# A state-space layer's kernel spectrum, placed and transformed in two halves of heads

## Chip, cores, metric

One core of a Trainium2 chip. The metric is the device time of one execution in microseconds, median of the runs shown; lower is better.

## What is computed

Two layers over `x` of shape (4, 1024, 128). Layer 0 adds to `x` a long convolution (state-space kernel `K` of 128 heads, applied by FFT, then a layer norm) and a mixture of 8 experts with the top 2 per token; layer 1 adds an attention and a second mixture. The change lies in the first part of layer 0:

```python
dtA = exp(log_dt)[:, None] * (-exp(log_A_real) + 1j * A_imag)      # (128 heads, 64 states)
K = 2 * real(einsum('hn,hnl->hl', Ct, exp(dtA[:, :, None] * arange(1024))))
Xf = rfft(xn, n=2048, axis=1);  Kf = rfft(K, n=2048, axis=1)
y = irfft(Xf * Kf.T[None], n=2048, axis=1)[:, :1024]
out = layernorm(xn + y + xn * D) * ln_w + ln_b
x = x + out + experts(xn)           # silu(xn W1) * (xn W2) W3, top 2 of 8, gated
```

## The kernel before, in words

The program is written engine by engine; within an engine the order of the code is the order of execution, and semaphores (`wait_ge`, `then_inc`) tie the engines together. Nothing is reordered by a scheduler.

**Opening.** SyncE loads `x` in eight groups of rows; TensorE turns them, VectorE takes means and variances, ScalarE normalises (`xn`). VectorE picks each token's two experts; GpSimd scatters the token rows into slots sorted by expert (`x_slots`, 64 indirect stores) from 36 us on.

**Token spectra.** The convolution of length 1024 is done as transforms of two row groups (c = 0, 1) of 512 rows each. `spectra(n)`, n = 0 to 15, multiplies the table `fwd0` (loaded into `acc[:, 0:4]`) with two row tiles of 4 x 128 columns into one of four PSUM banks; `spectrum_copy(n)` on ScalarE moves it into `z`. Even and odd halves stand apart, and `spectrum_sums()` on VectorE later combines them, in 4 instructions for each of the two frequency groups m and the two row groups, 16 in all.

**Tables of K.** VectorE builds powers `low` and `high` by doubling, `doublings(0)` for heads of chunks 0 and 1 and `doublings(1)` for chunks 2 and 3. Between them it writes the low parts of the experts' weights (`w0_low(e)`), each after ScalarE's high part (`w0_high(e)`), each after SyncE's load into `wraw`, which again waits for a low part two experts earlier. TensorE multiplies chunk c of `high` and `low` (L1983, contraction of 64 rows, two row halves in turn), ScalarE copies the result into `k_out` (`k_copy(c)`). Ahead of chunk 2 stand 8 products on `ident` whose results nobody reads.

**Placing and transforming K.** When all four chunks are copied, TensorE brings K into time order with 16 products on the 0/1 matrix `place` (L1999: contraction of 32 rows, 256 columns, four products in a row on the same 32 rows). ScalarE copies to `k_t`, TensorE transforms with `fwd0` (`khat_product(n)`, n = 0 to 3, four products of 256 columns each), ScalarE copies to `khat`, VectorE combines (`khat_sums`, `khat_parts`).

**Chunks.** Behind this the first layer's experts run over 19 chunks of 512 tokens: per chunk `turn_inputs` (turn), `up` (L1897 to 1899, three products per fp32 pair of high and low parts), `Silu`, `hid`, `down` (L2040). The first `up(0, 0, 0)` needs `khat_product` issued, the turned tokens split by ScalarE (`input_high`) and VectorE (`input_low`), and the first weight load; SyncE's loads of tokens and weights start when `chunk_tables()` has written the chunk order (products L1991, `order_turned`). During the chunks VectorE works off 96 products of the spectra (`product(i)`) in 15 turns, share `2 * PAIR * n // TURNS`; SyncE's load of `inv` in turn 13 waits for 88 of them, and the pieces of layer 1's weights, which ScalarE splits before it copies the last chunk's output, come behind it on SyncE's queue.

## Time and profile before

| | us |
|---|---|
| median of 3 runs | 796.37 |
| lowest, highest | 796.05, 797.06 |
| the profiled execution | 795.81 |
| its span, first to last instruction | 794.1 |
| TensorE busy in it | 748.0 (94%) |
| VectorE busy | 663.9 (84%) |
| ScalarE busy | 544.6 (69%) |
| GpSimd busy | 144.1 (18%) |

The shares are over the whole span. The stages differ: TensorE is idle for long stretches before 92 us and busy without a gap in the chunk loop. In the rows, a matmul in fp32 counts as two records, and times are from the first instruction on.

### The profile page before, as it was taken

What the parts mean: (1) busy time and instruction counts of PE and PEld (TensorE: products, weight loads), DVE (VectorE), ACT (ScalarE), POOL (GpSimd) and SP (SyncE); (2) the same over time, 40 slices, a digit from 0 to 9 for tenths busy, and PEclk for the clock granted to TensorE, in tenths of its full rate; (3) what the DMA queues carried; (4) which work ended last, traced back from release to release, by engine and by line L of the source; (5) the groups of instructions that cost most, each with busy time, mean ns of one, the idle gap of its engine ahead of it and who ended that gap; (6) DMA issues with size and microseconds to landing.
All of it is one profiled execution on the core that took longest, in us unless ns stands there. A gap on an engine that the chain in (4) does not pass through costs nothing.

```text
span 794.1 us, 11901 instructions
## 1 busy us (share of the span) xinstructions
PE 748.0 (94%) x3911; PEld 602.1 (76%) x3911; DVE 663.9 (84%) x1591; ACT 544.6 (69%) x934; POOL 144.1 (18%) x138
## 2 busy tenths in 40 slices
PE   9694599999999979999999999999999999999998
PEld 4343478888886447678888888888888887999997
DVE  7899989999378799998999899869777679777775
ACT  5971244444343578788998899889999996756663
POOL 0177772000000716324070000000000000000000
PEclk9797899999999999999999999999999999999999
DMA  9884377898764106132233122122221100000000
GB/s 307 330 276 161 140 240 227 261 303 279 228 194 156 50 8 133 31 100 54 60 86 63 41 50 51 46 48 43 53 48 46 51 16 1 14 21 14 21 15 28
DMA packets 81277, 85.24 MB, mean 107 GB/s; under 512 B 7361, under 2 KB 59841, under 8 KB 80961
## 3 DMA queue, kind: packets, MB, share of 16 engines
q1 hardware_dynamic: 76672, 75.93, 32.9%
q0 software_dynamic: 4096, 8.40, 3.7%
q8 instruction: 31, 0.51, 0.3%
q14 instruction: 30, 0.24, 0.1%
q10 hardware_dynamic: 448, 0.17, 0.1%
HBM read 59.17 MB, written 25.30 MB: 106 GB/s over the span
## 4 chain that ended last, share of the span: by engine, by line
PE 73%; DVE 19%; issue 2%; ACT 2%; DMA 2%; POOL 1%; SPq 0%; DVEq 0%; POOLq 0%; ACTq 0%
PE ps L1897 20%; PE ps L1899 19%; PE ps L1898 19%; PE ps L2040 5%; PE ps L2264 3%; DVE hid_lo L1823 2%; DVE xn L1498 1%; PE ps L2291 1%; POOL gate_row L685 1%; PE ps L2019 1%; PE ps L2010 1%; DMA wraw<-w 1%; DVE stats L988 1%; ACT xn L722 1%; DMA wst<-w 1%
## 5 line engine op out<-in xcount | busy, mean ns | idle before, releaser
L1823 DVE TENSOR_TENSOR hid_lo<-hid,hid_hi 128x512 fp32r<-128x512 f32 x256 | 175.9, 688 | 44.7 <-ACT hid_hi L912 41.8
L911 ACT ACTIVATE hid<-ps,b_sb 128x512 f32<-128x512 f32 x256 | 176.7, 690 | 45.1 <-PE ps L1899 25.5
L912 ACT ACTIVATE hid_hi<-ps,b_sb 128x512 fp32r<-128x512 f32 x256 | 174.7, 682 | 0.0
L1897 PE MATMUL ps<-hid_hi,w_lo 128*128 128x512 f32 x256 | 101.4, 396 | 5.3 <-DVE hid_lo L1823 5.3
L1897 PE MATMUL ps<-xt_hi,w_lo 128*128 128x512 f32 x256 | 102.3, 400 | 1.8 <-DVE xn L1490 1.8
L1899 PE MATMUL ps<-xt_hi,w_hi 128*128 128x512 f32 x256 | 100.0, 390 | 0.0
L1899 PE MATMUL ps<-hid_hi,w_hi 128*128 128x512 f32 x256 | 99.8, 390 | 0.0
L1898 PE MATMUL ps<-xt_lo,w_hi 128*128 128x512 f32 x256 | 99.7, 389 | 0.0
L1898 PE MATMUL ps<-hid_lo,w_hi 128*128 128x512 f32 x256 | 99.7, 389 | 0.0
L820 ACT ACTIVATE act<-ps 128x512 f32<-128x512 f32 (+1 forms) x57 | 34.0, 596 | 75.1 <-PE ps L1899 75.0
L685 POOL DMA_INDIRECT u_both<-y_slots,slot x56 | 64.7, 1155 | 85.4 <-DVE hid_lo L1823 69.6
L662 POOL DMA_INDIRECT x_slots<-xn,slot x64 | 69.1, 1080 | 53.1 <-DVE pairs L1177 33.9
L1897 PEld LDWEIGHTS ps<-hid_hi,w_lo 128*128 128x128 f32 x256 | 48.0, 188 | 21.1 <-DVE hid_lo L1823 11.1
L2040 PEld LDWEIGHTS ps<-wd,hid 128*128 128x128 f32 (+1 forms) x456 | 58.1, 191 | 3.7
L2040 PE MATMUL ps<-wd,hid 128*128 128x128 f32 (+1 forms) x456 | 59.7, 274 | 0.0
L706 ACT ACTIVATE pt_hi<-ps 128x512 fp32r<-128x512 f32 x64 | 35.0, 598 | 35.3 <-PE ps L2264 35.3
L1332 DVE TENSOR_TENSOR hid<-act,ps 128x512 f32<-128x512 f32 (+1 forms) x57 | 39.0, 683 | 22.1 <-ACT act L820 21.8
L1897 PEld LDWEIGHTS ps<-xt_hi,w_lo 128*128 128x128 f32 x256 | 48.1, 188 | 11.8 <-DVE xn L1490 2.2
L1899 PEld LDWEIGHTS ps<-xt_hi,w_hi 128*128 128x128 f32 x256 | 48.1, 188 | 10.4
L1899 PEld LDWEIGHTS ps<-hid_hi,w_hi 128*128 128x128 f32 x256 | 48.0, 188 | 10.4
L1815 DVE TENSOR_REDUCE sm<-ps 128x1 f32<-128x1024 f32 x32 | 39.2, 1224 | 19.6 <-PE ps L1899 19.2
L1898 PEld LDWEIGHTS ps<-hid_lo,w_hi 128*128 128x128 f32 x256 | 48.1, 188 | 9.5
(367 smaller groups left out, 1530.6 us busy)
## 6 DMA issues: line engine op xcount, KB each, us to landing
gate_row<-gates_dram SPq DMA_DIRECT2D x64, 256.0 KB, 4.9
wc<-w_split SPq DMA_DIRECT2D x57, 256.0 KB, 3.3
w_split<-wc SPq DMA_DIRECT2D x8, 768.0 KB, 4.4
x_slots<-prod SPq DMA_DIRECT2D x11, 512.0 KB, 7.6
xc<-x_slots SPq DMA_DIRECT2D x19, 256.0 KB, 3.6
y_slots<-yo SPq DMA_DIRECT2D x19, 256.0 KB, 3.1
wst<-w SPq DMA_DIRECT2D x16, 256.0 KB, 4.4
wd<-w SPq DMA_DIRECT2D x19, 192.0 KB, 4.4
```

The source lines that it names most:

```text
L662: nc.gpsimd.indirect_dma_start(x_slots, bass.IndirectOffsetOnAxis(ap=slot[:, k, t:t + 1], axis=0), rows_of_tile(t), None).then_inc(block_i ...
L685: nc.gpsimd.indirect_dma_start(dst, None, y_slots, rows_of).then_inc(signal, 16)
L706: copy = lambda dst, src: nc.scalar.activation(dst, src, ACT.Copy)
L911: nc.scalar.activation(hid1[:, u % 4], ps[:, u % 4], ACT.Gelu_apprx_tanh, bias=b1_sb[:, u:u + 1])
L912: nc.scalar.activation(hid1_hi[:, u % 4], ps[:, u % 4], ACT.Gelu_apprx_tanh, bias=b1_sb[:, u:u + 1]).then_inc(hid1_done, 1)
L1332: tt(hid[0:f, j], act[0:f, r], ps[0:f, 2 + r], mul).then_inc(hid_done, 1)
L1815: v = step.mark(nc.vector.reduce_max(sm[:, s, 0:1], ps[:, 2 * (n % 2):2 * (n % 2) + 2].rearrange("p a w -> p (a w)"), AX.X))
L1823: tt(hid1_lo[:, u % 4], hid1[:, u % 4], hid1_hi[:, u % 4].bitcast(F32), sub).then_inc(hid1_lo_done, 1)
L1897: mm(dst, a_lo, b_hi, start=first, stop=False)
L1898: mm(dst, a_hi, b_lo, start=False, stop=False)
L1899: return mm(dst, a_hi, b_hi, start=False, stop=last)
L2040: last = mm(ps[:, 4 + s, tokens], hid[0:f, j, tokens], wd[0:f, s, j * P:(j + 1) * P], start=(j == 0 and t == 0), stop=(j == J0 - 1 and t = ...
```

## The change

K is placed and transformed in two halves d = 0, 1 of 64 heads each. The host orders the heads so that chunks 0 and 1 are the heads 0 to 63, chunks 2 and 3 the rest. TensorE's new order: spectra 0 to 13, chunks 0 and 1, spectra 14 and 15, `place_product(0)`, the four `khat_product(0, n)`, chunk 2, the products of the chunk order, chunk 3, `place_product(1)`, the four `khat_product(1, n)` with the first `turn_inputs` after the first of them. Each placing or transforming product has 128 columns instead of 256, and the placing loop now has the row block `a` innermost. `k_t` moves to `acc[:, 6:8]`.

The spectra of the second row group (n = 8 to 15) take four row tiles instead of two; for one of the two halves some of the tables are the negated ones in `minus0`, a new input of 0.5 MB, loaded behind `fwd0`. So their even and odd parts come out combined, and `spectrum_sums(0)` on VectorE does the first row group alone. The 8 products on `ident` are gone. VectorE fills `place` behind `doublings(0)`. The share of products per turn is `min(13 * n // 2, 96)`, and GpSimd waits for an arrived block one tile earlier.

```diff
-                if t % BT == 1 and t > BT:
+                if t % BT == 0 and t:
                     block_arrived(t // BT - 1)
...
             sp.dma_start(fwd0, dft_fwd).then_inc(fwd0_in, 16)
+            sp.dma_start(minus0, dft_minus).then_inc(fwd0_in, 16)
...
+            k_t_copy(0)
+            act_e.wait_ge(w0_lo_done, E)
+            for n in range(M):
+                khat_copy(0, n)
+            k_copy(2)
+            k_copy(3)
+            k_t_copy(1)
...
-            def spectrum_sums():
+            def spectrum_sums(row_group):
 
                 dve.wait_ge(spectra_copied, 16)
-                for c in range(2):
+                for c in (row_group,):
...
-                upto_turn = lambda n: 2 * PAIR * n // TURNS
+                upto_turn = lambda n: min(13 * n // 2, 2 * PAIR)
...
-                    for i in range(2):
-                        t = 2 * odd + i
-                        last = mm(for_batch(ps[:, n % 4]), fwd0[:, t, part_, m * P:(m + 1) * P], rows3(c * CT + t),
-                                  start=(i == 0), stop=(i == 1))
+                    tiles = (0, 1, 2, 3) if c == 1 else (2 * other, 2 * other + 1)
+                    for t in tiles:
+                        from_minus = c == 1 and other and t // 2 != part_
+                        table = minus0[:, t % 2] if from_minus else fwd0[:, t]
+                        last = mm(for_batch(ps[:, n % 4]), table[:, part_, m * P:(m + 1) * P], rows3(c * CT + t),
+                                  start=(t == tiles[0]), stop=(t == tiles[-1]))
...
+            def place_product(d):
+                pe.wait_ge(k_copied, 4 * d + 4)
+                pe.wait_ge(spectra_copied, 16)
+                pe.wait_ge(place_done, 1)
+                if d:
+                    pe.wait_ge(khat_copied, M)
+                    pe.wait_ge(slots_done, 5)
+                for i in range(HG):
+                    for a in range(HG):
+                        block = slice(a * LO, (a + 1) * LO)
+                        last = mm(ps[:, a, d * P:(d + 1) * P], place[block, (3 - i) * LO:(7 - i) * LO],
+                                  k_out[block, d * 2 * G:(d + 1) * 2 * G, a * LO + i * G:a * LO + (i + 1) * G],
+                                  start=(i == 0), stop=(i == HG - 1))
...
             for c in range(KC):
                 if c == 2:
-                    pe.wait_ge(k_copied, 4)
-                    pe.wait_ge(spectra_copied, 16)
-                    for _ in range(8):
-                        mm(ps[:, 0, 0:2 * P], ident[:], fwd0[:, 0, 0, 0:2 * P], start=True, stop=True)
+                    spectra(range(SPECTRA_FIRST, 16))
+                    place_product(0)
+                    for n in range(M):
+                        khat_product(0, n)
+                if c == 3:
+                    pe.wait_ge(order_done, 1)
+                    pe.wait_ge(khat_copied, M)
+                    for i in range(3):
+                        last = mm(ps[0:1, 0, i * NC:(i + 1) * NC], of_chunk[:, i:i + 1], order_f[:], start=True, stop=True)
+                    last.then_inc(order_turned, 1)
```

The order of instructions at three places follows; line numbers are those of each kernel's own text. TensorE from ahead of chunk 2 (`ps<-high,low`) on, before:

```order
L1974 MATMUL ps<-acc,ident 128x256 [waits spectra_copied,k_copied]
L1974 MATMUL ps<-acc,ident 128x256 x7
L1983 MATMUL ps<-high,low 128x128 [waits k_copied,tables_done]
L1983 MATMUL ps<-high,low 128x128 x15
L1983 MATMUL ps<-high,low 128x128 [waits k_copied,tables_done]
L1983 MATMUL ps<-high,low 128x128 x15
L1991 MATMUL ps<-order_f,of_chunk 1x23 [waits k_copied,order_done]
L1991 MATMUL ps<-order_f,of_chunk 1x23 x2
L1999 MATMUL ps<-prod,place 128x256 [waits spectra_copied,k_copied,place_done]
L1999 MATMUL ps<-prod,place 128x256 x15
L2010 MATMUL ps<-half_way,acc 128x256 [waits k_t_copied]
```

The same place now (`prod` holds `k_out`, the second operand of L2014 lies in `acc` like the first):

```order
L2001 MATMUL ps<-prod,place 128x128 [waits place_done,spectra_copied,k_copied]
L2001 MATMUL ps<-prod,place 128x128 x15
L2014 MATMUL ps<-acc 128x128 [waits k_t_copied]
L2014 MATMUL ps<-acc 128x128 x15
L2038 MATMUL ps<-high,low 128x128 [waits k_copied,tables_done]
L2038 MATMUL ps<-high,low 128x128 x15
L2028 MATMUL ps<-order_f,of_chunk 1x23 [waits khat_copied,order_done]
L2028 MATMUL ps<-order_f,of_chunk 1x23 x2
L2038 MATMUL ps<-high,low 128x128 [waits k_copied,tables_done]
L2038 MATMUL ps<-high,low 128x128 x15
L2001 MATMUL ps<-prod,place 128x128 [waits khat_copied,place_done,slots_done,spectra_copied,k_copied]
L2001 MATMUL ps<-prod,place 128x128 x15
```

One half of placing and transforming moved ahead of chunk 2, and the products of the chunk order moved between chunks 2 and 3.

ScalarE from the copy of spectrum 6 (`z<-ps`) on, with the high parts of experts 4 to 7 (`wc<-wraw`), before:

```order
L706 ACTIVATE z<-ps 128x512 [waits spectra_mm] x10
L706 ACTIVATE wc<-wraw 128x3x256 [waits w0_stored0,wraw_in0]
L706 ACTIVATE wc<-wraw 128x3x256 [waits w0_stored1,wraw_in1]
L706 ACTIVATE wc<-wraw 128x3x256 [waits w0_stored0,wraw_in0]
L706 ACTIVATE wc<-wraw 128x3x256 [waits w0_stored1,wraw_in1]
L706 ACTIVATE prod<-ps 128x512 [waits k_mm_done,spare_out,blanks_out]
L706 ACTIVATE prod<-ps 128x512 [waits k_mm_done] x7
L706 ACTIVATE half_way<-ps 128x2x32x8 [waits k_t_done] x2
```

And now:

```order
L709 ACTIVATE z<-ps 128x512 [waits spectra_mm] x2
L709 ACTIVATE wc<-wraw 128x3x256 [waits w0_stored0,wraw_in0]
L709 ACTIVATE z<-ps 128x512 [waits spectra_mm]
L709 ACTIVATE wc<-wraw 128x3x256 [waits w0_stored1,wraw_in1]
L709 ACTIVATE z<-ps 128x512 [waits spectra_mm] x5
L709 ACTIVATE prod<-ps 128x512 [waits k_mm_done,spare_out,blanks_out]
L709 ACTIVATE prod<-ps 128x512 [waits k_mm_done] x3
L709 ACTIVATE wc<-wraw 128x3x256 [waits w0_stored0,wraw_in0]
L709 ACTIVATE z<-ps 128x512 [waits spectra_mm]
L709 ACTIVATE wc<-wraw 128x3x256 [waits w0_stored1,wraw_in1]
L709 ACTIVATE z<-ps 128x512 [waits spectra_mm]
L709 ACTIVATE acc<-ps 128x4x16x8 [waits k_t_done]
```

The high parts of experts 6 and 7 now stand behind the copies of chunks 0 and 1, that of expert 7 also behind the copy of spectrum 14.

VectorE in turn 13 of the chunk loop, from the chunk's third `hid` (85 rows) to its next chunk's second; products 86 and 87, counted from 0, are the pair `z<-prod`. Before:

```order
L1332 TENSOR_TENSOR hid<-act,ps 85x512 [waits act_done]
L1379 TENSOR_TENSOR prod<-z,khat 128x512 [waits products_done]
L1383 TENSOR_TENSOR prod<-prod 128x512 [waits products_done]
L1331 ISA
L1332 TENSOR_TENSOR hid<-act,ps 128x512 [waits act_done]
L1383 TENSOR_TENSOR prod<-prod 128x512 [waits products_done]
L1387 TENSOR_TENSOR z<-prod 128x512 [waits products_done] x2
L1331 REGISTER_ALU
L1332 TENSOR_TENSOR hid<-act,ps 128x512 [waits act_done]
```

And now:

```order
L1355 TENSOR_TENSOR hid<-act,ps 85x512 [waits act_done]
L1406 TENSOR_TENSOR prod<-prod 128x512 [waits products_done] x2
L1354 ISA
L1355 TENSOR_TENSOR hid<-act,ps 128x512 [waits act_done]
L1410 TENSOR_TENSOR z<-prod 128x512 [waits products_done] x2
L1387 TENSOR_TENSOR z<-z 128x512 [waits products_done]
L1354 REGISTER_ALU
L1355 TENSOR_TENSOR hid<-act,ps 128x512 [waits act_done]
```

The pair moved one product nearer to the `hid` ahead of it.

## Rows read from the trace of the kernel before

**Rows 1.** Chain of waits, 60 to 120 us: start, duration, what, records.
```profile
82.44 1.83 DVE wc L1222 x2
...
91.21 0.70 DVE high L1303
91.96 3.84 PE ps L1983 x64
...
97.02 4.89 PE ps L1999 x32
101.93 1.08 ACT half_way L706
103.06 1.99 PE ps L2010 x8
105.05 0.44 PE ps L2019 x4
105.49 5.18 PE ps L2010 x24
```

**Rows 2.** Stages: window, length, busy by engine with records, granted clock, DMA share, GB/s.
```profile
62.30:70.90 8.60, 0.00 (x0) 0.00 (x1) 8.53 (x16) 2.06 (x3) 6.46 (x8) 0.76 0.14 46
70.90:77.00 6.10, 6.07 (x56) 6.10 (x58) 5.96 (x33) 0.00 (x0) 4.88 (x5) 0.50 0.82 272
...
87.30:92.00 4.70, 2.19 (x12) 1.58 (x11) 4.67 (x10) 0.00 (x0) 3.48 (x5) 1.00 0.40 136
...
121.00:160.00 39.00, 39.00 (x251) 33.75 (x250) 38.08 (x63) 17.73 (x33) 3.11 (x3) 1.00 0.84 248
230.00:246.00 16.00, 16.00 (x102) 13.67 (x101) 15.55 (x27) 7.00 (x13) 0.00 (x0) 1.00 0.46 132
```

**Rows 3.** Timeline of TensorE: start, duration, line, operands, records, idle before and releaser.
```profile
51.70 10.57 PE L1952 MATMUL ps<-xn,acc 128*128 128x512 f32 x24 [0.60 <-ACT z L706]
70.93 6.71 PE L1983 MATMUL ps<-high,low 64*128 64x128 f32 x64 [8.66 <-issue]
...
95.73 0.31 PE L1991 MATMUL ps<-order_f,of_chunk 128*1 128x23 f32 x6
...
110.32 0.58 PE L1897 MATMUL ps<-xct_hi,wc 128*128 128x512 f32 x1
```

**Rows 4.** Timelines of VectorE, SyncE's queue and ScalarE, end of the chunk loop.
```profile
243.36 1.29 DVE L1387 TENSOR_TENSOR z<-prod 128x512 f32<-128x512 f32 x2
244.67 0.34 SPq L569 DMA_DIRECT2D prod<-dft_inv  x1
251.99 0.63 ACT L706 ACTIVATE w_hi<-wst 128x512 fp32r<-128x512 f32 x1 [4.84 <-DMA wst<-w]
```

**Rows 5.** Timeline of VectorE around the end of the tables.
```profile
93.88 0.24 DVE L1212 TENSOR_SCALAR order_f<-consts,place_f 128x23 f32<-128x23 f32 x1
...
94.38 0.38 DVE L1442 TENSOR_REDUCE place<-ident 128x32 f32<-128x128 f32 x1
...
97.12 0.68 DVE L1342 TENSOR_TENSOR z<-z 128x512 f32<-128x512 f32 x1
...
107.41 0.69 DVE L1327 TENSOR_TENSOR xct_lo<-ps,xct_hi 128x512 fp32r<-128x512 f32 x1
```

**Rows 6.** Timeline of ScalarE: the high part of expert 7, the last copies to `k_out`.
```profile
81.47 0.84 ACT L706 ACTIVATE wc<-wraw 128x768 fp32r<-128x768 f32 x1 [3.50 <-DMA wraw<-w]
...
95.83 1.09 ACT L706 ACTIVATE prod<-ps 128x512 f32<-128x512 f32 x2 [0.70 <-PE ps L1983]
```

**Rows 7.** Timeline of SyncE's queue: the load of expert 7, the first weights.
```profile
73.58 0.50 SPq L501 DMA_DIRECT2D wraw<-w  x1
...
101.26 1.39 SPq L528 DMA_DIRECT2D wc<-w_split  x3
```

**Rows 8.** DMA view, 0 to 130 us: transfer, count, KB each, median us to landing.
```profile
wc<-w_split SPq DMA_DIRECT2D x14, 256.0 KB, 3.6
...
acc<-dft_fwd SPq DMA_DIRECT2D x1, 1024.0 KB, 9.8
```

More of the change, by code:

```diff
@@ L42 @@
 STATIC_PAIRS = MIN_PAIRS - 2
+SPECTRA_FIRST = 14
 TURNS = 1 + 2 * STATIC_PAIRS + 4
@@ L730, in spectrum_copy @@
             def spectrum_copy(n):
-                c, m, part_, odd = spectrum(n)
+                c, m, part_, other = spectrum(n)
                 act_e.wait_ge(spectra_mm, n + 1)
-                copy(z[:, m + HM * odd, c, part_], ps[:, n % 4]).then_inc(spectra_copied, 1)
+                copy(z[:, m + HM * other, c, part_], ps[:, n % 4]).then_inc(spectra_copied, 1)
             def w0_high(e):
@@ L1315, in _ @@
             doublings(0)
+            dve.wait_ge(ident_done, 1)
+            dve.wait_ge(ranked, 1)
+            v = step.mark(nc.vector.memset(place[:], 0.0))
+            need(v)
+            nc.vector.reduce_sum(place[:, 3 * LO:4 * LO], ident.rearrange("p (a n) -> p n a", a=HG), AX.X).then_inc(place_done, 1)
             w0_low(4)
@@ L1436, in weights_low @@
                 tt(w_lo[:, col:col + cols], wst1[:, n % STAGES, 0:cols], w_hi[:, col:col + cols].bitcast(F32), sub).then_inc(w1_lo_done, 1)
-            dve.wait_ge(ident_done, 1)
-            dve.wait_ge(ranked, 1)
-            v = step.mark(nc.vector.memset(place[:], 0.0))
-            need(v)
-            nc.vector.reduce_sum(place[:, 3 * LO:4 * LO], ident.rearrange("p (a n) -> p n a", a=HG), AX.X).then_inc(place_done, 1)
             chunk_tables()
             gates0()
-            spectrum_sums()
+            spectrum_sums(0)
             dve.wait_ge(rows_in, 80)
@@ L1942, in spectra @@
                 for n in numbers:
-                    c, m, part_, odd = spectrum(n)
+                    c, m, part_, other = spectrum(n)
                     if n >= 4:
@@ L1965, in _ @@
             mm(ps[:, 7, 0:T * E], before[:], chosen, start=False, stop=True).then_inc(ranked, 1)
-            pe.wait_ge(fwd0_in, 16)
-            spectra(range(16))
+            pe.wait_ge(fwd0_in, 32)
+            spectra(range(SPECTRA_FIRST))
             pe.wait_ge(ws_lo_done, 1)
+            k_halves = k_t.rearrange("p (c t) h -> p t c h", c=2)
+            def place_product(d):
[11 more added lines that the diff above has]
+                                  start=(i == 0), stop=(i == HG - 1))
+                        if i == HG - 1:
+                            last.then_inc(k_t_done, 1)
@@ new lines, in khat_product @@
+            def khat_product(d, n):
+                m, odd = divmod(n, 2)
+                bank, at = khat_at(d, n)
+                if n == 0:
+                    pe.wait_ge(k_t_copied, d + 1)
+                for part_ in range(2):
+                    for i in range(2):
+                        last = mm(ps[:, bank, at + part_ * P:at + (part_ + 1) * P], fwd0[:, 2 * odd + i, part_, m * P:(m + 1) * P],
+                                  k_halves[:, 2 * odd + i, :, d * HH:(d + 1) * HH], start=(i == 0), stop=(i == 1))
+                last.then_inc(khat_mm, 1)
@@ L1985, in _ @@
                                 last.then_inc(k_mm_done, 1)
[L1988 to L2013 removed]
+            place_product(1)
             def turn_inputs(q, k, s):
```

99 lines of the change are left out of this document (40 added, 59 removed).

## Prediction

> **What bounds the kernel now.** I read the chain of waits first, over the stretch from 60 to 112 us, because every line of the diff but one acts there. Up to 91.91 us it runs through VectorE: the doubling tables of the second 32 heads, with the splits of the expert weights between them [rows 1]. VectorE has no gap there that matters (5.96 of 6.10 us busy, 8.53 of 8.60 [rows 2]). From 91.96 us it is a ladder on which TensorE and ScalarE take turns: products of chunks 2 and 3 (3.84), copies, placing (4.89), copy (1.08), transform (1.99 and 5.18 with the turning of the first tokens, 0.44, between), and at 110.32 us the first expert product [rows 1, 3]. That is 18.4 us in which one engine waits for the other. The second thing to see is that TensorE has nothing to do for long stretches ahead of the ladder: no instruction from 62.3 to 70.9 us, and a granted clock of 0.50, the 1.2 GHz level, when it starts again [rows 2]. The third is what comes behind: from 121 to 160 us TensorE is busy 39.00 of 39.00 us [rows 2], so whatever time the ladder gives back moves the whole chunk loop forward. Last I read the end of the loop, 230 to 246 us, where VectorE is busy 15.55 of 16.00 us [rows 2] and a load that waits for its products leads to the last output and the first gather [rows 4].
>
> **The ladder, step by step.** The change does half of the placing and transforming (heads of chunks 0 and 1) before the last tables are ready, so behind them only the other half stands. I follow the new ladder from its start to the first expert product, which was at 110.32.
>
> Start. VectorE's two instructions that fill `place` move from behind `order_f` to ahead of the weight split of experts 4 and 5. They run from 94.12 to 94.76 [rows 5], so they cost 0.64 us on the bounding engine: the tables end at 92.55 and TensorE starts at 92.60 instead of 91.96.
>
> Products of chunks 2 and 3. They took 3.84 us for 64 records, 0.060 each [rows 1]. Chunk 2 ends at 92.60 + 1.92 = 94.52. Now the three small products for the chunk order stand between the chunks and wait for `order_f`, which was ready at 93.88 + 0.24 = 94.12 [rows 5] and is now at 94.76. Six records of theirs start within 0.2 us or so (six took 0.31 with the tail of the last [rows 3]), so chunk 3 runs from 95.0 to 96.9. The wait holds up only TensorE; what is queued behind it is chunk 3, and behind that everything on the ladder. It costs 0.5 us, and in return the tables for SyncE come about 0.9 us earlier.
>
> Copies to `k_out`. From the end of the products to the first placing product it was 95.80 to 97.02, 1.22 us with two copies of 1.09 in all [rows 1, 6]. The same now: 98.1.
>
> Placing. Before: 16 products with 256 columns, 32 records, 4.89 us, 0.153 each [rows 1]; four products in a row use the same 32 rows of the array. Now 16 products with 128 columns, and neighbours use different row groups. No row shows that. One bound is a strictly serial pace: a transform record with 256 columns takes 7.17 / 32 = 0.224 us [rows 1], so one with 128 columns 0.112, and 32 of them 3.6 us. The nearest row is that of the `k` products, the same 128 columns and two row groups in turn, 0.060 a record, so 1.92 us. The other bound is four groups at once, 3.6 / 4 = 0.9 us. I take 1.92, since shape and alternation are those of that row: placing ends at 100.0.
>
> On this the Trainium skill speaks too (TensorEngine Tiling (Array Packing), Performance Considerations and Key Properties): a contraction of 32 rows or fewer can go four tiles wide, since tiles load weights and multiply independently. By that the step would be 0.9 us and the sum 1.0 us better; no row here shows four groups, so I keep two. The same section speaks against the change: a change of the tiling mode drains the engine, and the new order switches between 64, 128 and 32 rows oftener. The row at 95.73 differs: the 128-row products follow the 64-row products with no idle time recorded before them [rows 3]. By the row it costs nothing; were there a drain it would add to the ladder.
>
> Copy to `k_t`. One ScalarE copy of 512 elements a partition was exposed behind the placing, 101.93 to 103.06 with its hand-overs, 1.13 [rows 1]. The new copy has 512 elements too: 101.2.
>
> Transform. 32 records of 0.224 us and 0.44 for the turning made 103.06 to 110.32 [rows 1, 3]. Now half the columns: 3.58 + 0.44 = 4.0, so the first expert product can start at 105.2. Its inputs: VectorE's `xct_lo` stood at 107.41, behind 16 `spectrum_sums` that begin at 97.12 [rows 5], ready but never late. Had those 16 stayed, `xct_lo` would now end near 107 and hold TensorE by 2 us; with the eight of row group 0 VectorE is free near 102. So that part of the change gives nothing by itself and is what lets the rest through. The gain at the first expert product is 110.32 - 105.2 = 5.1 us: -2.97 placing, -3.26 transform, +0.64, +0.5.
>
> **What has to be hidden.** TensorE now has to finish the first half before 92.60. Spectra 8 and up have four products, eight records at 0.44 us [rows 3] instead of four: spectrum 9 ends near 54.6, 13 near 68.7. So the idle time ahead of 70.93 shrinks from 8.6 to about 2.2 us; a pause of 2.5 us inside 87.3 to 92.0 left the clock at 1.00 [rows 2]. At that clock chunks 0 and 1 take 3.84 and not 6.71 us [rows 1, 3]: 74.8. Spectra 14 and 15 are 3.52 each: 78.3 and 81.8. ScalarE copies 15 only after the split of expert 7, whose load it had to wait for until 81.47 [rows 6] and which is 0.64 later now: 83.0, copied 83.6. Placing 1.92, copy 1.13, transform 3.58: 90.2. The cover is 2.4 us; beyond it each microsecond costs one. VectorE wants the split of expert 7 at about 84.0 (second of the two at 82.44 plus 0.64 [rows 1]); margin 1.0. The eight products on `ident` ahead of chunk 2 go, at no price. The new 0.5 MB load of `minus0` follows the 1 MB of `fwd0`, which landed 9.8 us after its issue among other loads [rows 8]; half as much data is 0 to 5 us more by that row, and the first spectra wait for it. I take 1, because it queues behind the same loads as `fwd0`; that comes out of the 2.2 us ahead of 70.93, and from there on each microsecond goes into the cover of 2.4. Weights: the first load was issued at 101.26 [rows 7] and lands in 3.6 us [rows 8]; 0.9 earlier that is 104.0, against a need at 105.2.
>
> **The end of the loop.** The share of the spectrum products becomes 13n//2 a turn. In turn 13 the product that the load of `inv` waits for, number 88, comes as second behind the middle `hid` and not as third, so SyncE's 244.67 comes 0.60 us earlier (VectorE does two in 1.29 with the tail of the second), and with it the piece of weights that ScalarE waits 4.84 us for until 251.99, the last output behind that piece and the gather [rows 4]. Between 0 (were the piece late for another reason) and 1.2 us (two products); I take 0.6. That GpSimd waits for a landed block one tile earlier I price at nothing, since no step of the ladder waits for GpSimd [rows 1]; were the first token load late for it, that would take from the 1.2 us that the weights have left.
>
> **The sum.** 5.1 + 0.6 = 5.7 us. The profiled execution took 795.81 us, 794.1 of it span; it would be 790.1. It lies 0.56 under the median of the three runs, 796.37, and I forecast for the median: 796.37 - 5.7 = 790.7.
>
> **Rivals.**
> A. Placing runs four row groups at once: 1.0 less, 789.7. For it: 32 rows; against: no row shows more than two at once.
> B. Part of the gain is not there: placing stays serial (+1.7, 792.4), or the first weights come late. The load issued at 73.58 was waited for until 81.47, 7.9 us [rows 6, 7]; one like it would hold the first product by 3 us, 793.7.
> C. The gain goes into a new wait: `minus0` or the loads of experts 6 and 7 come so late that tables and first half end 4 to 6 us later, 795 to 797. Against it: the margins of 1.0 to 2.4 us above, and traffic of the same size as before from 70 to 83 us.
> D. Slower: TensorE does the first half at 1.2 GHz. Chunks 0 and 1 then end at 77.6 as in the row, spectrum 14 at 84.7, so ScalarE's split of expert 7, now queued behind its copy, ends at 86.1 and VectorE stands; spectrum 15 ends at 91.7, placing at 96.2, copy at 97.3, transform at 104.5, 11.9 us past 92.60: 790.7 + 11.9 = 802.6. It costs from 2.4 us on and is slower than before from 5.7 us past 92.60 on. For it: the clock was 0.50 for 6 us at this place [rows 2]. Against it: that followed 8.6 us without work, which is filled now, and the clock rose within 6 us of work.
>
> **How the numbers follow.** Forecast 0.62, A 0.10, B 0.14, C 0.08, D 0.06. Faster by over 0.2% (1.6 us, about what a measurement of this kernel tells from no change) are the forecast, A, B and a little of C: 0.88. Within 0.2%: most of C, 0.06. Slower: D, 0.06. The range goes from 789.0 (A with the upper end of the tail) to 793.4 (B with serial placing and 1 us of a missed cover); C and D, 0.14, and the worst of B lie outside.
>
> **What would show it.** In the changed profile: placing as two stretches, the second about 1.9 us long; the second transform 4.0 us with the turning; the last tables at 92.6; the first expert product at 105; granted clock 1.00 from 70.9; SyncE's `inv` load 5.7 us earlier. The forecast is wrong if the first half ends after 92.6, if `xct_lo` or a weight load is what the first expert product waits for, or if the chunk loop shows new idle time on TensorE.

## Result, and the profile after

The changed kernel takes 790.3 us (median of 4 runs, 789.29 to 790.4) against 796.21 us of the kernel before on the same chip (4 runs, 795.25 to 797.06): a ratio of 0.9917, 95% interval 0.9896 to 0.9938. I had forecast 790.7. The sum is right to half a microsecond, but its two terms are not: counted alike, the ladder gave less than I had worked out and the end of the loop three times as much.

The profiled execution's span is 788.6 us; before it was 794.1. TensorE in the stretch of the ladder, its timeline, columns as in [rows 3]:

```profile
72.06 3.84 PE L2038 MATMUL ps<-high,low 64*128 64x128 f32 x64 [2.57 <-issue]
75.84 7.13 PE L1972 MATMUL ps<-xn,acc 128*128 128x512 f32 x16
83.92 1.17 PE L2001 MATMUL ps<-prod,place 32*128 32x128 f32 x32 [0.95 <-issue]
86.34 3.84 PE L2014 MATMUL ps<-acc 128*128 128x128 f32 x32 [1.25 <-ACT acc L709]
93.74 2.68 PE L2038 MATMUL ps<-high,low 64*128 64x128 f32 x32 [3.56 <-DVE high L1321]
96.36 0.39 PE L2028 MATMUL ps<-order_f,of_chunk 128*1 128x23 f32 x6
96.68 2.86 PE L2038 MATMUL ps<-high,low 64*128 64x128 f32 x32
100.71 1.17 PE L2001 MATMUL ps<-prod,place 32*128 32x128 f32 x32 [1.17 <-ACT prod L709]
103.15 1.16 PE L2014 MATMUL ps<-acc 128*128 128x128 f32 x8 [1.27 <-ACT acc L709]
104.15 0.60 PE L2048 MATMUL ps<-ident,xc 128*128 128x128 f32 x4
104.58 2.84 PE L2014 MATMUL ps<-acc 128*128 128x128 f32 x24
107.18 0.48 PE L1915 MATMUL ps<-xct_hi,wc 128*128 128x512 f32 x1
```

The shape is the forecast one: the first half of placing and transform lies ahead of chunk 2, with 3.56 us to spare, chunks 0 and 1 take 3.84 us and not 6.71 [rows 3], and the second placing and transform are short. Against it stand chunks 2 and 3: 2.68 and 2.86 us for 32 records each, where 1.92 were due. The stages show why (columns as in [rows 2]):

```profile
90.20:93.70 3.50, 0.00 (x0) 0.00 (x0) 3.46 (x8) 0.38 (x1) 2.58 (x4) 1.00 0.24 75
93.70:95.00 1.30, 1.26 (x22) 1.26 (x24) 1.26 (x12) 0.00 (x0) 0.99 (x2) 0.99 0.20 63
95.00:98.40 3.40, 3.40 (x38) 3.09 (x36) 2.38 (x16) 1.09 (x2) 2.70 (x3) 0.50 0.19 60
98.40:99.60 1.20, 1.14 (x20) 0.95 (x18) 1.20 (x3) 0.03 (x1) 0.98 (x1) 1.00 0.17 55
```

TensorE has no work from 90.2 to 93.7 us, and from 95.0 to 98.4 its granted clock is 0.50, the 1.2 GHz level.

The two executions also began differently, which hides part of the gain. VectorE's write of the tokens' slots, which ends the routing and comes ahead of every line of the diff that matters here, stands 1.23 us later in the changed kernel. The timeline of the kernel before, TensorE and VectorE:

```profile
6.27 1.02 PE L1913 MATMUL ps<-prod,wg_centred 128*8 128x512 f32 x2
...
35.28 0.20 DVE L1169 CAST slot<-slot_f 128x64 int32<-128x64 f32 x1
```

and that of the changed kernel:

```profile
6.73 1.88 PE L1931 MATMUL ps<-prod,wg_centred 128*8 128x512 f32 x2
...
36.51 0.20 DVE L1187 CAST slot<-slot_f 128x64 int32<-128x64 f32 x1
```

The same two products of the routing took nearly twice as long, which is what the lower clock makes of the products of chunks 0 and 1 elsewhere; the rows give 1.00 for this first stretch in both profiles, so I read the pace from the durations. It comes with the execution: one program below (the version with unused products as fillers) has this write at 36.41 us in one profile and at 35.22 in the other. How often each kernel starts late is not shown: the three profiles of the kernel before and of a version of it have the write at 34.9 to 35.3, the two of the changed kernel at 36.5, and versions of the changed kernel at both. So I count from that write on (us behind it; "due" is the prediction's own ladder, less 35.28; the last column, e11, is the version without fillers at the end of the experiments):

| | before | due | changed | e11 |
|---|---|---|---|---|
| last tables end | 56.63 | 57.27 | 57.18 | 56.49 |
| products of chunk 3 end | 60.52 | 61.62 | 63.03 | 60.83 |
| placing ends | 66.62 | 64.72 | 65.37 | 63.17 |
| first expert product | 75.04 | 69.92 | 70.67 | 68.47 |
| load of `inv` on SyncE | 209.39 | 203.67 | 204.33 | 202.13 |
| first Gelu of the next part | 248.40 | 242.70 | 242.21 | 239.85 |
| end | 758.77 | 753.07 | 752.13 | 749.89 |

The rows of the tail, the changed kernel's load of `inv` and first Gelu (timelines of SyncE's queue and ScalarE), then the first Gelu of the kernel before:

```profile
240.84 0.34 SPq L572 DMA_DIRECT2D prod<-dft_inv  x1
278.72 0.67 ACT L929 ACTIVATE hid<-ps,b_sb 128x512 f32<-128x512 f32 x1
```

```profile
283.68 0.67 ACT L911 ACTIVATE hid<-ps,b_sb 128x512 f32<-128x512 f32 x1
```

Like for like the two profiles differ by 6.6 us: 4.4 up to the first expert product, 0.7 from there to the load of `inv`, 1.1 from that load to the first Gelu, and 0.4 behind it, for which no cause was looked for.

### The profile page after: what moved, and what is told of

Read it like the earlier page. It is cut to its first block, busy times and chain, and to the rows that moved or that the text cites. A ratio compares the mean times of both kernels' runs of the same rounds, so it can differ in the third digit from the quotient of the medians.

```text
span 788.6 us, 12059 instructions
## 1 busy us (share of the span) xinstructions
PE 756.0 (96%) x3991; PEld 603.6 (77%) x3991; DVE 658.5 (83%) x1583; ACT 544.5 (69%) x938; POOL 145.3 (18%) x138
## 4 chain that ended last, share of the span: by engine, by line
PE 75%; DVE 16%; DMA 3%; ACT 2%; issue 2%; POOL 1%; SPq 0%; DVEq 0%; ACTq 0%; POOLq 0%
PE ps L1915 20%; PE ps L1917 20%; PE ps L1916 20%; PE ps L2069 6%; PE ps L2291 3%; DVE hid_lo L1841 2%; DVE xn L1516 1%; PE ps L1931 1%; PE ps L2318 1%; PE ps L2048 1%; POOL gate_row L688 1%; DMA wraw<-w 1%; ACT xn L725 1%; PE ps L2038 1%; DVE wc L1240 1%
## 5 line engine op out<-in xcount | busy, mean ns | idle before, releaser
L665 POOL DMA_INDIRECT x_slots<-xn,slot x64 | 71.1, 1111 | 55.9 <-DVE pairs L1195 35.1
L709 ACT ACTIVATE pt_hi<-ps 128x512 fp32r<-128x512 f32 x64 | 35.0, 598 | 35.3 <-PE ps L2291 35.3
L1355 DVE TENSOR_TENSOR hid<-act,ps 128x512 f32<-128x512 f32 (+1 forms) x57 | 38.9, 682 | 21.4 <-ACT act L840 21.0
L1833 DVE TENSOR_REDUCE sm<-ps 128x1 f32<-128x1024 f32 x32 | 39.1, 1223 | 19.6 <-PE ps L1917 19.2
```

The costliest lines, as they stand in the source:

```text
L665: nc.gpsimd.indirect_dma_start(x_slots, bass.IndirectOffsetOnAxis(ap=slot[:, k, t:t + 1], axis=0), rows_of_tile(t), None).then_inc(block_i ...
L709: copy = lambda dst, src: nc.scalar.activation(dst, src, ACT.Copy)
L1355: tt(hid[0:f, j], act[0:f, r], ps[0:f, 2 + r], mul).then_inc(hid_done, 1)
L1833: v = step.mark(nc.vector.reduce_max(sm[:, s, 0:1], ps[:, 2 * (n % 2):2 * (n % 2) + 2].rearrange("p a w -> p (a w)"), AX.X))
```

## Experiments

**Is it the pause ahead of chunk 2?** The eight products on `ident` that the change takes away ahead of chunk 2, priced by me at nothing, could have kept the clock up. Seven of them, called fillers below, were put back behind the first half:

```
                     for n in range(M):
                         khat_product(0, n)
+                    for _ in range(7):
+                        mm(ps[:, 7, 0:2 * P], ident[:], fwd0[:, 0, 0, 0:2 * P], start=True, stop=True)
```

> Seven products of 256 columns on the identity (results unused, to a PSUM bank that is free there) stand on TensorE behind the first half's transform and ahead of chunk 2, where the changed kernel is idle from 90.2 to 93.7 us and then runs the products of chunks 2 and 3 from 95.0 to 98.4 at a granted clock of 0.50. Theory: the idle time is what brought the clock down, and the eight products that the change removed from this place, which I had priced at nothing, kept it up. Then with the seven the clock stays at 1.00, chunk 2 takes 1.92 us instead of 2.62, chunk 3 1.92 instead of 2.85, and the first expert product comes 1.2 to 1.6 us earlier (with a start like that of the changed kernel's profile near 105.7 instead of 107.18): 790.3 - 1.4 = 788.9. Rival 1: the slow pace comes from the three products of the order between the chunks and the turn from 64 to 128 and back to 64 rows; then pace and time stay (790.3). Rival 2: the clock falls all the same, the seven only delay chunk 2: 790.3 to 791.

Measured: 790.61 us (789.26 to 791.2), no gain over 790.3. The theory is half right. TensorE's timeline and its stages in this run:

```profile
93.61 2.06 PE L2040 MATMUL ps<-high,low 64*128 64x128 f32 x32 [0.52 <-DVE high L1321]
96.00 0.31 PE L2030 MATMUL ps<-order_f,of_chunk 128*1 128x23 f32 x6 [0.34 <-DVE order_f L1230]
96.24 2.06 PE L2040 MATMUL ps<-high,low 64*128 64x128 f32 x32
99.46 1.17 PE L2001 MATMUL ps<-prod,place 32*128 32x128 f32 x32 [1.17 <-ACT prod L709]
101.91 2.08 PE L2014 MATMUL ps<-acc 128*128 128x128 f32 x8 [1.27 <-ACT acc L709]
```

```profile
101.40:104.80 3.40, 2.89 (x13) 2.89 (x14) 1.32 (x3) 0.46 (x1) 2.49 (x4) 0.50 0.86 263
```

The chunks run at full pace (2.06 with the tail of the last record), so the products of the order were not what slowed them. But the stretch of 0.50 is still there, 6.4 us later, behind two pauses of 1.2 us in which TensorE waits for ScalarE's copies, and it now slows the transform: the first 8 records take 2.08 us and not 1.16. It also shows the wait for `order_f` that the slow clock hides in the changed kernel: 0.34 us.

**Placing over the row groups in turn, or one after the other.**

```
-                for i in range(HG):
-                    for a in range(HG):
+                for a in range(HG):
+                    for i in range(HG):
```

> Only the order of the 16 placing products is put back: four in a row on the same 32 rows, then the next 32. Theory: the second placing took 1.17 us (32 records, 0.037 each) because neighbours lie in four different row groups; in series a record of 128 columns is half of the 0.153 of 256 columns to 0.112, so 2.4 to 3.6 us, and the first expert product comes 1.2 to 2.4 us later: 791.5 to 792.7. The first half has 3.5 us of cover and hides its own part. Rival: the placing was short because it has 128 columns and not because of the row groups; then it stays near 1.2 to 1.6 and the time at 790.3 to 790.7.

Measured: 792.82 us (791.95 to 795.36). The second placing in its timeline:

```profile
98.99 2.98 PE L2001 MATMUL ps<-prod,place 32*128 32x128 f32 x32 [1.17 <-ACT prod L709]
```

2.98 us against 1.17, but the last 0.47 us of it lie in a stretch of 0.50 that starts at 101.5 us. The first placing of the same run had the clock at 1.00 throughout:

```profile
83.70 2.79 PE L2001 MATMUL ps<-prod,place 32*128 32x128 f32 x32 [1.17 <-issue]
```

So at the same clock the order over the four row groups is worth 1.6 us, a factor of 2.4. The stretch also takes in the transform, so the first expert product is 2.6 us later (73.30 behind the routing) and not 1.6 to 1.8. By the Trainium skill (TensorEngine Tiling (Array Packing), Theoretical Speedup) the gain of 32-row tiles is up to four times. The runs show 2.4. The Trainium skill also names a drain at a change of the tiling mode (same page, Key Properties). The timelines show no idle time for it between 64-row and 128-row products (96.24 above).

**The same order alone, in the kernel before.**

```
-            for a in range(HG):
-                block = slice(a * LO, (a + 1) * LO)
-                for i in range(HG):
+            for i in range(HG):
+                for a in range(HG):
+                    block = slice(a * LO, (a + 1) * LO)
...
-                if a % 2:
-                    last.then_inc(k_t_done, 1)
+                    if i == HG - 1 and a % 2:
+                        last.then_inc(k_t_done, 1)
```

> The kernel before with one line's order changed: the 16 placing products go over the four row groups in turn, as in the changed kernel; no halves, no negated tables, nothing moved. It tells what this order alone is worth. Theory: 32 records of 256 columns at twice the changed kernel's 0.037 us take 2.3 to 2.4 us instead of 4.89. But both copies to k_t, of which the first lay beside the placing, now stand behind it, 1.08 us more, so the first expert product comes about 1.5 us earlier: 796.4 - 1.5 = 794.9. Rival: it stays at 4.9 us, since 256 columns fill the array's columns whatever the rows: no gain, or 1 us lost by the copy, 797.5.

Measured: 794.63 us (793.64 to 797.27), beside 797.81 for the kernel before, measured with it (795.47 to 801.26); ratio 0.9959, interval 0.9936 to 0.9981. Placing took 2.01 us, a factor of 2.4 for 256 columns too, and the copy behind it costs about what was expected (TensorE waits 2.06 us, before 1.16, so 0.9 of the expected 1.08):

```profile
96.89 2.01 PE L1999 MATMUL ps<-prod,place 32*128 32x256 f32 x32 [0.98 <-issue]
100.95 3.68 PE L2010 MATMUL ps<-half_way,acc 128*128 128x256 f32 x8 [2.06 <-ACT half_way L706]
```

In the profiled execution a stretch of 0.50 from 101.0 to 104.4 ate most of the gain (first expert product 74.65 us behind the routing, before 75.04); in the median the one line is worth 3.2 us, by the interval 1.5 to 5.1.

**Half the sums on VectorE.** The last step of my ladder rests on VectorE being free in time because TensorE now does the second row group's sums.

```
-                for c in (row_group,):
+                for c in range(2):
```

> VectorE does the sums of both row groups again, 16 instead of 8, over the spectra that TensorE has already combined (so the second row group is summed twice and its spectrum is another one); TensorE's work stays. It prices the VectorE side of the negated tables. In the changed kernel VectorE is free at 102.9 and xct_lo runs at 105.48, 1.1 us before the first expert product can need it. Theory: eight more sums of 0.60 us end at 107.7, xct_lo ends at 108.4, and TensorE's second product, which needs it, starts 1 us or a little more later: first to third expert product later by 0.9 to 1.3 us, time 791.2 to 791.6. The khat sums behind them come 2.2 us later and hold nothing. Rival: the spectrum products in the chunk loop, of which VectorE has 38.0 of 39.0 us full, come later by 4.8 us and never catch up, and the loop's end comes later too: 793 to 795. Rival: no effect, 790.3, if something else holds TensorE until 108.

Measured: 793.1 us (791.57 to 794.54). `xct_lo` follows the sums without a gap and TensorE waits for it; VectorE, then TensorE:

```profile
106.45 0.68 DVE L1370 SCALAR_TENSOR_TENSOR z<-z 128x512 f32<-128x512 f32 x1
107.06 0.28 DVE L1465 TENSOR_SCALAR vec_rows<-vec_rows 128x128 f32<-128x128 f32 x1
107.37 0.69 DVE L1350 TENSOR_TENSOR xct_lo<-ps,xct_hi 128x512 fp32r<-128x512 f32 x1
```

```profile
108.11 0.50 PE L1915 MATMUL ps<-xct_hi,wc 128*128 128x512 f32 x1 [1.00 <-DVE xct_lo L1350]
```

Up to here it costs the expected microsecond; counted from the routing 0.7 are left, since this run's tables came 0.5 us earlier. Up to its end the run loses 1.75 us against the changed kernel (753.88 against 752.13): another 0.3 in the chunk loop, 0.3 behind the load of `inv`, 0.4 behind the first Gelu. The median lies 2.5 us above that of the run with the seven products, measured beside it. So it is 1 us at the place and 2 or a little more in all; what makes the rest was not taken apart.

This run also bears on the pause ahead of chunk 2, which was 2.68 us in it and not 3.56. The clock fell all the same, from 94.9 to 98.3 us:

```profile
93.41 2.48 PE L2038 MATMUL ps<-high,low 64*128 64x128 f32 x32 [2.68 <-DVE high L1321]
```

**What the longer spectra do for the clock.** The other side of the same edit:

```
-                    tiles = (0, 1, 2, 3) if c == 1 else (2 * other, 2 * other + 1)
+                    tiles = (2 * other, 2 * other + 1)
```

> TensorE's spectra of the second row group have two tiles each again, without the sums that belong to it (the second row group's even and odd parts stay uncombined, so its spectrum is another one); VectorE's work stays. It tells what the longer spectra do for the clock. Theory: TensorE is then idle from about 63.5 to 72 us, chunks 0 and 1 run at a granted clock of 0.50 as in the kernel before (6.7 us instead of 3.84). They end near 78.8; spectra 14 and 15 are 1.8 us each instead of 3.5, so the copy of spectrum 15 still waits for the split of expert 7 (load until 82.5) and the first half ends near 90.2 to 91 as now, inside the 3.5 us of cover: 790.3. Rival (D of the prediction): the clock falls again behind chunks 0 and 1, as it did at 80.4 us in the kernel before, placing and transform run at half pace (2.3 and 7.7 us instead of 1.17 and 3.84) and the first half ends near 95.3: 1.6 us past the tables, 791 to 792.5, less what a warm clock in chunks 2 and 3 then gives back.

Measured: 790.24 us (789.27 to 792.56), the changed kernel's time. TensorE's timeline:

```profile
70.97 6.68 PE L2038 MATMUL ps<-high,low 64*128 64x128 f32 x64 [9.25 <-issue]
...
84.31 2.09 PE L2001 MATMUL ps<-prod,place 32*128 32x128 f32 x32 [3.02 <-issue]
...
92.81 2.06 PE L2038 MATMUL ps<-high,low 64*128 64x128 f32 x32
```

This is rival D in a milder form: the clock is at 0.50 from 66.7 to 77.0 and again from 83.8 to 90.6 us, chunks 0 and 1 take 6.68 us and the first placing 2.09. Yet chunk 2 starts only 0.5 us behind its tables, since the clock comes back in between and the cover is larger than I had it. I had priced D at 11.9 us by letting the low level hold from 70.9 to the end of the first half, and with spectra twice as long. With these two-tile spectra it costs 0.5. With the long ones the low level was met here for 3.4 us only (70.7 to 74.1, in a profile with fillers below), and the first half still ended ahead of the tables.

**The share of the spectrum products in a turn.**

```
-                upto_turn = lambda n: min(13 * n // 2, 2 * PAIR)
+                upto_turn = lambda n: 2 * PAIR * n // TURNS
```

> Only the share of the spectrum products in each turn of the chunk loop is put back. It prices the term of the tail. From the first expert product to SyncE's load of inv the changed kernel took 0.69 us less than the kernel before (133.66 against 134.35 us), and from there to the first Gelu of the next part 1.1 us less. Theory: the 0.6 us come from the pair of products that moved one place forward, so here the first stretch is 134.3 us again, while the rest of the tail, the weight piece and the gathers, does not depend on it: 790.3 + 0.6 = 790.9. Rival: the whole tail hangs on it, by the time at which the gathers meet other transfers: 134.3 and 39.0 us, 791.9.

Measured: 790.78 us (one run), 134.30 us from the first expert product to the load of `inv` and 38.98 from there to the first Gelu: the rival holds. The time is only half a microsecond above the changed kernel's because this execution started early (the write of the slots at 34.98 us). Counted from the routing it ends 1.9 us later (754.04 against 752.13), 1.7 of them between the first expert product and the first Gelu, for an edit of which I had the price at 0.6. GpSimd's gathers of the first outputs, in the timeline of this run and then of the changed kernel's second profile:

```profile
256.23 1.44 POOL L688 DMA_INDIRECT gate_row<-y_slots,slot  x1 [0.30 <-issue]
257.97 1.49 POOL L688 DMA_INDIRECT gate_row<-y_slots,slot  x1 [0.30 <-issue]
259.77 0.94 POOL L688 DMA_INDIRECT gate_row<-y_slots,slot  x1 [0.30 <-issue]
```

```profile
256.90 0.94 POOL L688 DMA_INDIRECT gate_row<-y_slots,slot  x1 [0.30 <-issue]
258.14 0.94 POOL L688 DMA_INDIRECT gate_row<-y_slots,slot  x1 [0.30 <-issue]
```

Two of the eight gathers are half a microsecond longer, and each of the two lies over a 128x512 instruction of VectorE with two operands from SBUF (this run, VectorE):

```profile
255.57 1.28 DVE L1459 TENSOR_TENSOR w_lo<-wst,w_hi 128x512 fp32r<-128x512 f32 x2
...
257.99 0.66 DVE L1550 TENSOR_TENSOR xn<-xn,vec_rows 128x512 f32<-128x512 f32 x1
```

The Trainium skill (GPSIMD Engine Reference, Specifications) says that GpSimd shares its SBUF interfaces with VectorE and names VectorE instructions with two SBUF inputs among those that contend. The rows agree in what they pair; but in the second profile of the changed kernel the gather at 256.90 lies over the same instruction and stays at 0.94, so what decides is finer than an overlap. VectorE there:

```profile
256.29 1.33 DVE L1459 TENSOR_TENSOR w_lo<-wst,w_hi 128x512 fp32r<-128x512 f32 x2
```

Read instruction by instruction, the fourth gather of all fourteen profiles sorts itself by when a `w_lo` starts beside it. Where one starts 0.02 to 0.07 us ahead of the gather, the gather takes 1.43 to 1.48 us (five profiles). Where one starts within 0.01 us of it, the gather takes 0.94 or 0.95 us and that `w_lo` 0.71 to 0.73 instead of 0.68 (three). Where one starts 0.10 to 0.35 us behind it, the gather takes 1.00 to 1.25 us (six). This is a pattern of the rows; no run took the collision by itself.

**The kernel before once more, and the changed kernel once more.**

> The kernel before once more, for a second profile of it: how much of the difference between the two profiles is chance. Theory: the start up to the end of the routing (35.28 us before, 36.51 in the changed kernel) differs between executions of one kernel by a microsecond, because the granted clock rises at another time; from the end of the routing to the first expert product it is 75.0 us again, from that to the load of inv 134.35 again. From that load to the first Gelu it was 39.0 us and 37.9 in the changed kernel: if that is the change's, 39.0 again; if it is chance of the gathers, anything from 37.8 to 39. Time 795 to 797.

> The changed kernel once more, for a second profile. Theory: TensorE's granted clock falls to 0.50 for 3.4 us or more somewhere between 85 and 106 us, since all six kernels with the unfilled pauses of the ladder showed that (at 95.0, 101.4, 87.9 and 101.5, 94.9, 100.9, 92.8 us), and its place differs from execution to execution; the first expert product comes 70 to 73 us behind the end of the routing (70.7 in the first profile). From the first expert product to the load of inv 133.67 us again. Time 790.3. Rival: the stretch at 95.0 to 98.4 is fixed by the program and is there again, within a tenth of a microsecond of the start of chunk 2.

Measured: 799.56 us (one run) and 790.34 us (790.24 to 790.57). The changed kernel repeats to a tenth: start 36.50, a stretch of 0.50 from 94.8 to 98.2, first expert product 70.73 us behind the routing, 133.67 to the load of `inv`; my expectation that the stretch wanders was wrong for this kernel. The kernel before doesn't repeat. Its second profile has a stretch of 0.50 from 99.6 to 109.8 us, where the first had none:

```profile
96.30 6.34 PE L1999 MATMUL ps<-prod,place 32*128 32x256 f32 x32 [0.97 <-issue]
```

Placing took 6.34 and not 4.89 us [rows 1], the first expert product comes at 79.13 us behind the routing and not 75.04. From there to the load of `inv` it is 134.36 again, and from that to the first Gelu 39.13 (39.01 in the first). So the profile on which I built the sum was a lucky one: four medians of the kernel before, taken at different times, are 796.2, 797.3, 796.4 and 797.8 us, its runs lie from 794.8 to 801.3, while the eight runs of the changed kernel lie between 789.3 and 790.6.

**All pauses filled, and a version to beat both.** Two of the fillers also behind chunk 3 and two behind the second placing:

> Beside the seven products on the identity ahead of chunk 2, two of them stand behind chunk 3 and two behind the second placing, where TensorE waits 1.2 us each time for a copy of ScalarE. With the seven alone the stretch at a granted clock of 0.50 did not go away but moved from 95.0 to 98.4 on to 101.4 to 104.8, from the products of chunks 2 and 3 on to the transform, so the time stayed. Theory: the pauses of the ladder taken together bring the clock down, and with all three filled it stays at 1.00 to the first expert product, which then comes 1.3 to 1.6 us earlier than in the changed kernel, measured from the end of the routing (70.7 us behind it there, 69.2 now): 790.3 - 1.4 = 788.9. Rival: the stretch of 0.50 moves on once more, behind the first expert product or into it, and the time stays at 790.3. Rival: the fillers end late and delay what follows by up to 0.3 us each.

Measured: 790.16 us (788.09 to 793.53). The profiled execution is the slowest of the four and shows what fillers can't mend:

```profile
85.52 2.07 PE L2001 MATMUL ps<-prod,place 32*128 32x128 f32 x32 [2.28 <-issue]
88.81 5.55 PE L2014 MATMUL ps<-acc 128*128 128x128 f32 x32 [1.22 <-ACT acc L709]
94.19 3.19 PE L2025 MATMUL ps<-acc,ident 128*128 128x256 f32 x14
97.31 2.06 PE L2040 MATMUL ps<-high,low 64*128 64x128 f32 x32
```

The load of expert 7 came later here, the first placing waited 2.28 us for it, the clock fell to 0.50 from 85.6 to 92.4, and the first half ended level with the tables; the fillers then held chunk 2 for another 3.2 us.

The version has six, two and two fillers and three further edits: the fill of `place` ahead of `w0_low(0)`, where VectorE waits for ScalarE anyway, the order's products one quarter into chunk 3, and on SyncE the second token load behind the first expert's weights.

```
+            v = step.mark(nc.vector.memset(place[:], 0.0))
...
             w0_low(0)
...
+                    if c == 3 and i == 1:
+                        pe.wait_ge(order_done, 1)
...
-            for q in range(2):
-                x_load_early(q, q)
+            x_load_early(0, 0)
...
                 down_load(e, q)
+                if q == 0:
+                    x_load_early(1, 1)
```

> A version to beat both kernels: the fillers of the run before (six, two and two products), the two instructions that fill place at the head of VectorE's weight splits where it waits 1.3 us for ScalarE, the order's three products one quarter into chunk 3 (so that TensorE does not wait for order_f), and on SyncE the second token load behind the first expert's weights. Theory: 0.64 us for place, 0.3 for the order, 1.4 for the clock: first expert product 68.3 us behind the end of the routing instead of 70.7, time 790.3 - 2.4 = 787.9. Rival: the first weights become the wait; they land near 103 us of the profile, earlier by 1.7 us through the order on SyncE, else they would have been level with the need. Rival: the clock falls in the ladder all the same: 789.3.

> The version with filled pauses, place set up early, the order inside chunk 3 and the weights first, once more beside the changed kernel on the same chip. Theory: no stretch of 0.50 in the ladder, first expert product 68.3 us behind the end of the routing again, time 1 to 2 us under the changed kernel's of the same call. Rival: that its first profile had no such stretch was chance; then a stretch is there, and the time is within 0.8 us of the changed kernel's.

> The same version without the fillers: place set up early, order inside chunk 3, weights first. It tells the fillers' part. Theory: a stretch of 0.50 of 3.4 us or more is in the ladder again and costs 1.3 to 1.7 us; first expert product 69.6 to 70.1 us behind the end of the routing against 68.3 with the fillers, time 0.9 us under that of the changed kernel. Rival: the other three edits carry it all: 68.3 again.

Measured: 789.27 us (788.34 to 789.59) at first; later, all on one chip, 788.06 (787.56 to 788.61) with the fillers, 787.89 (786.94 to 791.25) without, and 790.34 for the changed kernel. So the version is 2.3 us faster than the changed kernel, and by the medians of four runs each the fillers are not what does it. Without them, TensorE's timeline in the profiled execution, the fastest of the four:

```profile
91.84 2.50 PE L2039 MATMUL ps<-high,low 64*128 64x128 f32 x40 [2.98 <-DVE high L1322]
94.27 0.31 PE L2032 MATMUL ps<-order_f,of_chunk 128*1 128x23 f32 x6
94.51 1.61 PE L2039 MATMUL ps<-high,low 64*128 64x128 f32 x24
97.28 1.17 PE L2002 MATMUL ps<-prod,place 32*128 32x128 f32 x32 [1.17 <-ACT prod L710]
```

and its stage:

```profile
91.80:103.80 12.00, 9.52 (x139) 8.97 (x139) 10.08 (x40) 4.88 (x9) 9.26 (x10) 1.00 0.57 171
```

The pauses are all there (2.98 and 1.17 in these rows), and the clock is at 1.00 to the end of the ladder; the first expert product comes 68.47 us behind the routing, against 68.32 and 69.42 in the two profiles with fillers. In the second of those a stretch of 0.50 from 70.7 to 74.1 made the first half late and the fillers held chunk 2 for another 1.3 us. The three edits are worth about a microsecond by their rows (0.69 us earlier tables, 0.3 for `order_f`); the rest of the 2.2 us at the first expert product is the clock. That the pause is 0.6 us shorter does not explain the clock, since behind the 2.68 us of the run with both sums it fell. Over the eleven profiles with the halved ladder the clock fell inside chunks 2 and 3 in four of the five with a pause of 2.7 to 3.6 us ahead of them, and in none of the six with 0.5 us or less. So the fall goes with a pause there, but the pause does not decide it alone; what else does stays open. The four runs of this version differ by 4.3 us.

## Why the prediction was right, point by point

**What bounds the kernel, and the shape of the ladder:** right. What the ladder gave went through to the end of the chunk loop: 133.66 us from the first expert product to the load of `inv` (before 134.35), with no new idle time on TensorE.

**Start:** right. Tables end 57.18 us behind the routing, due were 57.27; the 0.64 us for `place` are there.

**Chunks 2 and 3 and the order between them:** wrong by 1.5 us, the step that failed: 5.80 us instead of 4.3. I took the clock at 1.00 through the ladder from one row (a pause of 2.5 us that did not lower it [rows 2]) and priced the eight products on `ident` at nothing. By my own numbers the pause they leave ahead of chunk 2 was 2.4 us (90.2 to 92.6), no longer than in that row. It came out at 3.56, since the first half ended earlier than due; and one row was too little, since behind 2.68 us the clock fell too. The wait for `order_f`, priced at 0.5, is 0.15 to 0.34 us where the clock is up, and not visible where it is down.

**Placing:** 1.17 us, due 1.92 with 0.9 as the lower bound. Rival A was nearly it; I chose the row of two row groups, and four do more. From the end of chunk 3 to the end of the placing that gives 0.76 back.

**Copy and transform:** right, the transform 4.03 us against 4.02, the copy with its hand-overs 1.27 against 1.13.

**Sum at the first expert product:** 4.4 instead of 5.1 us.

**What has to be hidden:** right in kind and too cautious. The load of `minus0` delays nothing (spectra start 1.2 us later in the profile, as the routing does), the first half ends 3.5 us ahead of the tables, expert 7's split is ready for VectorE, and TensorE waits for no weights. Chunks 0 and 1 ran at full pace, so rival D did not happen. It is the load of expert 7 that can use the cover up, as in the run with filled pauses. GpSimd's earlier wait for an arrived block was not run by itself.

**The sums on VectorE:** right in kind. Without the halving TensorE waits for `xct_lo`; 2 us were due, it was 1.0 there and about 1.8 to the end.

**The end of the loop:** the pair moved one place and the load of `inv` came 0.60 to 0.71 us earlier in nine of the ten profiles with the new share, as worked out (0.60), and 0.36 in the one with all the sums on VectorE. But the term was mis-sized: 1.7 us by the run with the old share, 1.8 between the two first profiles, beyond my bound of 1.2. What I left out is what the earlier start does to the gathers. From the load of `inv` to the first Gelu it is 39.0 to 39.1 us in the four profiles with the old share and 37.7 to 38.2 in nine of the ten with the new one (38.9 in one). Between the two first profiles about 0.3 of that is the weight piece, and 0.85 lie behind the last output, where two gathers are half a microsecond longer in all four with the old share. The profile with 38.9 has the new share and both long gathers, so the share makes the collision likely or unlikely and does not rule it out.

So the sum fits by luck. Like for like the gain was 6.6 us and not 5.7: the ladder 0.7 short, the tail 1.2 over, and 0.4 behind the first Gelu that I had not forecast. The late start of the changed kernel's profile, 1.23 us, hides more than that surplus. Against the kernel before as it runs, with a median half a microsecond to two above the profile I used, the change is worth more than I said: 7.5 us when both were measured again on one chip.

## What to carry to other kernels

A term that rests on TensorE's pace needs the granted clock of its own stretch, and a pause that an edit opens or closes ahead of it belongs to the price. Small-row products that follow each other should lie in different row groups: one loop order was worth a factor of 2.4 on 32 rows. Where one profile is all there is, take the spread of its clock rows and starts as part of the range; count two profiles from a common event and not from zero.

## What the hardware showed that I had not expected

The same program shows stretches at a granted clock of 0.50 in other places from execution to execution: the kernel before has none between 87.2 us and the last output in one profile, and one from 99.6 to 109.8 in the other, worth 4 us. No length of a pause tells them apart here: behind 2.45 us without work there was one (70.7 us, the version with fillers), behind 2.57 none (72.06 us in the changed kernel); ahead of chunk 2 there was one behind 2.68 us (both sums on VectorE) and none behind 2.98 (e11). Filling one pause moved the stretch on and did not remove it. The first products of the routing run at one of two paces, seven profiles each, which shifts everything behind them by 1 to 2 us. An indirect gather on GpSimd took from 0.94 to 1.49 us beside VectorE instructions with two SBUF operands, and a few hundredths of a microsecond in their starts went with half a microsecond of its length.
